# Stacking a three-term split of queries and keys: 12 copies inside the SBUF in place of 32 selection matmuls and four reads per batch

## The reference

```python
def _L0_xattn_ref(q, k, v, w_q, b_q, w_k, b_k, w_v, b_v, w_o, b_o):
    def proj(x, w, b):
        return (x @ w.T + b).reshape(B, S, N_HEADS, D_K).transpose(0, 2, 1, 3)
    qh = proj(q, w_q, b_q); kh = proj(k, w_k, b_k); vh = proj(v, w_v, b_v)
    scores = jnp.einsum('bhqd,bhkd->bhqk', qh, kh) / jnp.sqrt(D_K)
    attn = jax.nn.softmax(scores, axis=-1)
    out = jnp.einsum('bhqk,bhkd->bhqd', attn, vh).transpose(0, 2, 1, 3).reshape(B, S, D_MODEL)
    return out @ w_o.T + b_o
...
x = x + jnp.tanh(g_xattn[0]) * _L0_xattn_ref(_layernorm(x), ctx_1024, ctx_1024, ...)
x = x + jnp.tanh(g_ffn[0]) * _L0_ffn_ref(_layernorm(x), ...)   # 8 experts, top 2, silu(g) * u
```

## Time and profile before

| | before |
|---|---|
| median of 3 runs | 1110.66 us (1105.49 to 1113.64) |
| the profiled execution's own time | 1108.67 us |
| its span, first to last instruction | 1107.0 us |
| mean granted TensorE clock | 0.956 |
| PE, PEld busy share of the span | 91%, 78% |
| DVE, ACT, POOL busy share of the span | 55%, 46%, 33% |
| one iteration of the loop (MT to MT) | 24.86 us |

### The profile page before, as it was taken

How to read it: one execution, slowest core, us unless ns; L and a number is a source line. 1 busy time by engine, 2 the same in 40 slices (tenths; PEclk the granted TensorE clock), 3 DMA queues, 4 the chain that set the end, 5 groups by cost and what they waited for, 6 DMA issues and landing times.

```text
span 1107.0 us, 24925 instructions
## 1 busy us (share of the span) xinstructions
PE 1009.7 (91%) x8750; PEld 860.1 (78%) x8750; DVE 610.4 (55%) x1525; ACT 504.3 (46%) x800; POOL 365.1 (33%) x439
## 2 busy tenths in 40 slices
PE   5899999999999987738999999999889999999994
PEld 4566777777777754527899999999689999999993
DVE  3657777778777773533644444444354444444442
ACT  4467777777777764322433232322243232332321
POOL 1224545555555553424212122121222222121221
PEclk9899999999999996868999999999989999999997
DMA  8001111111111155475612121121262122121211
GB/s 249 21 21 30 42 41 40 45 55 49 40 40 49 40 211 209 157 241 151 237 29 38 20 39 25 34 35 24 41 232 39 20 39 34 24 39 20 39 28 23
DMA packets 48365, 77.20 MB, mean 70 GB/s; under 512 B 8768, under 2 KB 42176, under 8 KB 44480
## 3 DMA queue, kind: packets, MB, share of 16 engines
q0 software_dynamic: 18080, 50.15, 16.8%
q1 hardware_dynamic: 30240, 26.47, 8.4%
HBM read 52.07 MB, written 24.26 MB: 69 GB/s over the span
## 4 chain that ended last, share of the span: by engine, by line
PE 79%; ACT 5%; DVE 4%; issue 4%; POOL 3%; DMA 2%; SPq 1%; POOLq 0%; ACTq 0%; DVEq 0%
PE gate L1514 16%; PE up L1514 16%; PE down L1527 11%; PE down L1529 6%; PE pv L587 4%; PE scores L576 4%; PE misc L483 4%; PE scores L537 3%; PE maxps L551 2%; PE misc L510 2%; PE misc L519 2%; ACT probs L767 2%; POOL K_rest L1200 2%; PE misc L621 1%; PE turned L1455 1%
## 5 line engine op out<-in xcount | busy, mean ns | idle before, releaser
L1805 POOL DMA_INDIRECT out<-y,token x64 | 99.8, 1559 | 437.8 <-DVE y L1712 350.3
L1607 ACT ACTIVATE silu<-gate 128x512 f32<-128x512 f32 x128 | 76.5, 598 | 280.9 <-PE up L1514 280.9
L1514 PE MATMUL gate<-x_hi,w_split 128*128 128x256 f32 x1024 | 186.0, 284 | 6.5 <-DVE w_split L1686 4.5
L976 DVE TENSOR_REDUCE max_neg<-maxps 128x4 f32<-128x1024 f32 x128 | 156.4, 1222 | 57.5 <-PE maxps L551 57.5
L1527 PE MATMUL down<-w_split,h_hi 128*128 128x512 f32 x512 | 185.8, 398 | 0.0
L1514 PE MATMUL up<-x_hi,w_split 128*128 128x256 f32 x1024 | 185.4, 283 | 0.0
L1703 DVE TENSOR_TENSOR h<-silu,up 128x512 f32<-128x512 f32 x128 | 88.0, 688 | 176.4 <-ACT silu L1607 176.4
L767 ACT ACTIVATE probs<-scores 128x1024 f32<-128x1024 f32 x124 | 127.3, 1026 | 78.3 <-PE scores L576 77.2
L1514 PEld LDWEIGHTS gate<-x_hi,w_split 128*128 128x128 f32 x1024 | 150.6, 191 | 10.1 <-issue 6.8
L1514 PEld LDWEIGHTS up<-x_hi,w_split 128*128 128x128 f32 x1024 | 149.6, 190 | 0.0
L1529 PE MATMUL down<-w_split,h_lo 128*128 128x256 f32 x512 | 144.1, 282 | 0.0
(11 more groups left out here) (205 smaller groups left out, 1595.7 us busy)
## 6 DMA issues: line engine op xcount, KB each, us to landing
stage<-gate_T POOLq DMA_DIRECT2D x10, 1024.0 KB, 6.4
stage<-up_T POOLq DMA_DIRECT2D x10, 1024.0 KB, 8.4
stage<-down_T POOLq DMA_DIRECT2D x10, 1024.0 KB, 10.3
xg<-dispatched SPq DMA_DIRECT2D x34, 272.0 KB, 3.0
ctxT<-ctxT SPq DMA_DIRECT2D x17, 256.0 KB, 3.0
x_all<-x SPq DMA_DIRECT2D x16, 256.0 KB, 5.1
out<-x_all SPq DMA_DIRECT2D x16, 256.0 KB, 2.2
dispatched<-pads SPq DMA_DIRECT2D x4, 272.0 KB, 13.7
```

The source lines that it names most:

```text
L976: V.tensor_reduce(to, maxps[:], AX.X, ALU.max, negate=True).then_inc(s["max_taken"], 1)
L1514: last = mm(bank[:, i, :], weights(w, mat)[:, c, cols], x[:, c, :], start=m == 0, stop=m == len(terms) - 1)
L1607: nc.scalar.activation(silu[pair % 2][:], gate[pair % 2][:], ACT.Silu).then_inc(s_silu, 1)
L1805: pool.indirect_dma_start(out, bass.IndirectOffsetOnAxis(token[:, t:t + 1], axis=0), y[:, t, :], None, compute_op=ALU.add).then_inc(s_adde ...
```

## The change

For batches 2 to 15 the four units are gone from PE and ACT. SP copies instead: `stack` on SP issues three DMAs (one per term) for each half `c` of Q and of K, 12 per batch, each 128 partitions x 1 KB of `high` or `rest` into every fourth partition of `queries` or `keys`. For that the rows of a stack are interleaved (row 4 * dim + term, `STEP` = 4), the host permutes the columns of the Q and K weights, and the shift row is row 63. M0 to M7 now contract 63 rows, of which each fourth holds zeros. On SP the first halves stand between `store_residual` and `store_shift`, behind waits for S3 and for the splits of K and Q; the second halves stand behind `store_shift` and a wait for S7. M0 and M4 wait for the halves (`stacked`), and so does the next `split` on POOL.

Batches 0 and 1 are still stacked by matmuls, now with 128-row selection matrices that lie in `ctx_high` and `ctx_rest` until these are needed; they are 1 MB to load in place of 0.5 MB.

The order is changed too. PE: TX goes ahead of S4, Q behind M4, S5 and M5 behind Q, then RK and weigh 1. ACT: `read_k` and `norm_x` go ahead of the exponentials of S3, the read of TX behind them, `read_q` ahead of those of S5, the read of TX2 ahead of those of S7. DVE's and POOL's orders stay.

```diff
-SHIFT = 3 * DK
+TERMS = 3
+STEP = 4
+SHIFT = STACK - 1
...
-        FULL = ["V", "TO0", "TO1", "K", "TN", "WO", "TX", "RK", "Q", "TX2", "LG", "MT"]
+        FULL = ["V", "TO0", "TO1", "K", "TN", "WO", "TX", "Q", "RK", "TX2", "LG", "MT"]
...
+        def picks_of(what):
+
+            held = (c_high[0], c_high[1]) if what == "Q" else (c_rest[0], c_rest[1])
+            return [part[:].rearrange("p c s -> p (c s)") for part in held]
...
-            load(((probs[0][:, :, 0, :], pick_rows),), "picks_loaded")
+            load(((probs[0][:], pick_rows),), "picks_loaded")
...
+            def stack(what, c, to):
+
+                for term, part in enumerate((high, rest, high) if what == "Q" else (high, high, rest)):
+                    sp.dma_start(to[term::STEP, c * BLOCKS:(c + 1) * BLOCKS].bitcast(fp32),
+                                 part[what][:, c].bitcast(fp32)).then_inc(stacked[what][c], 16)
...
                 if back:
                     store_residual(b - 1, use)
+                if ahead:
+                    sp.wait_ge(s["unit_written"], unit(b, f"S{BLOCKS - 1}") + 1)
+                    sp.wait_ge(s["k_split"], b + 3)
+                    stack("K", 0, k[par])
+                    sp.wait_ge(s["q_split"], b + 3)
+                    stack("Q", 0, q[par])
                 if nxt:
                     store_shift(b + 1, 1 - par, use)
+                if ahead:
+                    sp.wait_ge(s["unit_written"], unit(b, f"S{HPAIRS - 1}") + 1)
+                    stack("K", 1, k[par])
+                    stack("Q", 1, q[par])
...
-                for i in range(QT):
-                    for part, source in (("high", high), ("rest", rest)):
-                        for half in range(HPP):
-                            r = slice(half * STACK, (half + 1) * STACK)
-                            last = mm(scores[:, half * QT + i, :], picks[f"{what} {part}"][r, i, :], source[what][r, c, :],
-                                      start=part == "high", stop=part == "rest")
+                for i in range(BLOCKS):
+                    for m, source in enumerate((high, rest)):
+                        last = mm(scores[:, i, :], picks_of(what)[m][:, i * P:(i + 1) * P], source[what][:, c, :], start=m == 0, stop=m == 1)
...
-                if pair == 0:
-
-                    pe.wait_ge(s["unit_read"], units)
+                if isinstance(b, int) and b < 2:
+                    if pair == 0:
+
+                        pe.wait_ge(s["unit_read"], units)
+                elif pair % BLOCKS == 0:
+                    for what in "KQ":
+
+                        pe.wait_ge(stacked[what][pair // BLOCKS], b * STACKED - STACKED)
...
                 if back:
                     attn_out(use)
+                if ahead:
+                    turn_x(b + 2, use)
                 score(b, par, 4)
                 max_of_next(4)
                 if ahead:
-                    turn_x(b + 2, use)
+                    project_q(use)
+                score(b, par, 5)
+                max_of_next(5)
                 if is_last(b):
                     use.read(pe, "KNOWN")
                 if late:
                     ranks(b - 2, use)
-                stack_ahead("K0")
                 weigh(b, par, 1)
-                max_of_next(5)
-                score(b, par, 5)
-                if ahead:
-                    project_q(use)
                 score(b, par, 6)
...
-                stack_ahead("K1")
                 if back:
                     logits(use)
                 if nxt:
                     turn_maxima(b + 1, use)
-                stack_ahead("Q0")
                 weigh(b, par, 3)
-                stack_ahead("Q1")
...
                 exps(b, 2)
+                if ahead:
+                    read_k(b + 2, use)
                 if back:
                     read_whole(oT[:], "TN", use)
+                if ahead:
+                    norm_x(b + 2)
                 exps(b, 3)
                 if ahead:
-                    read_k(b + 2, use)
-                    norm_x(b + 2)
+                    read_whole(xT[:], "TX", use)
                 exps(b, 4)
...
                 if ahead:
-                    read_whole(xT[:], "TX", use)
-                stack_ahead("K0")
+                    read_q(b + 2, use)
                 exps(b, 5)
                 if back:
                     norm_x2(b - 1, 1 - par)
                 read_pv(b, 1)
                 exps(b, 6)
-                if ahead:
-                    read_q(b + 2, use)
-                exps(b, 7)
                 if back:
                     read_whole(x2T[:], "TX2", use)
+                exps(b, 7)
                 read_pv(b, 2)
-                stack_ahead("K1")
                 if back:
                     sigmoid(use)
-                stack_ahead("Q0")
-                stack_ahead("Q1")
                 read_pv(b, 3)
...
+                if isinstance(b, int) and b == 2:
+                    alone.wait_ge(s["unit_written"], 2 * len(STACKS))
+                else:
+                    for done in stacked[what]:
+                        alone.wait_ge(done, b * STACKED - 2 * STACKED)
                 G.tensor_copy(high[what][:], dense[what][:]).then_inc(s["high_chain"], 1)
```

More of the change, by code:

```diff
@@ L158, in attention_stage @@
         rest = {what: sb(f"{what}_rest", [P, HC, SEQ], f32r) for what in "QK"}
-        picks = {what: sb(f"picks_{what}", [P, QT, P], f32r) for what in ("Q high", "Q rest", "K high", "K rest")}
         q = [sb(f"queries{i}", [P, HPAIRS, SEQ], f32r) for i in range(2)]
@@ L279, in read @@
                 eng.wait_ge(misc_read[n], uses + 1)
-        UNITS = ["S0", "S1", "S2", "S3", "S4", "K0", "S5", "S6", "S7", "K1", "Q0", "Q1"]
+        def picks_of(what):
+            held = (c_high[0], c_high[1]) if what == "Q" else (c_rest[0], c_rest[1])
+            return [part[:].rearrange("p c s -> p (c s)") for part in held]
+        UNITS = [f"S{pair}" for pair in range(HPAIRS)]
         STACKS = ["K0", "Q0", "K1", "Q1"]
+        STACKED = 16 * TERMS
         def units_before(b):
-            last = isinstance(b, int) and b == BATCHES - 1
-            return b * len(UNITS) + (2 * len(STACKS) if not last else len(STACKS))
+            return b * len(UNITS) + 2 * len(STACKS)
         def unit(b, what):
-            order = [n for n in UNITS if n not in STACKS] if isinstance(b, int) and b >= BATCHES - 2 else UNITS
-            return units_before(b) + order.index(what)
+            return units_before(b) + UNITS.index(what)
         def is_last(b):
@@ L863, in body @@
             def body(b, par, use, ahead, nxt, back, late):
-                def stack_ahead(what):
-                    if ahead:
-                        read_stack(par, what[0], int(what[1]), unit(b, what))
                 exps(b, 0)
@@ L1064, in vector_attention @@
             for n, what in enumerate("QK"):
-                for m, part in enumerate(("high", "rest")):
-                    last = V.tensor_copy(picks[f"{what} {part}"][:], probs[0][:, 2 * n + m, 0, :].rearrange("p (i c) -> p i c", i=QT))
+                for m in range(2):
+                    last = V.tensor_copy(picks_of(what)[m], probs[0][:, 2 * n + m].rearrange("p t s -> p (t s)"))
             last.then_inc(s["picks_ready"], 1)
@@ L1241, in body @@
                 if ahead:
[L1242 removed]
+                    split(b + 2, "Q", use)
                 if late:
@@ L1259, in gpsimd_attention @@
             return scatter_next_to_last, scatter_last
-        handed = dict(over=attention_over, s=s, units=units_before(BATCHES - 1) + sum(n not in STACKS for n in UNITS))
+        handed = dict(over=attention_over, s=s, units=units_before(BATCHES - 1) + len(UNITS))
         return sync_attention, tensor_attention, scalar_attention, vector_attention, gpsimd_attention, handed
```

24 lines of the change are left out of this document (9 added, 15 removed).

## The result

The changed kernel takes **1133.25 us** (median of 4 runs, 1131.22 to 1135.36), the kernel before 1109.48 on the same chip: ratio **1.0221, 95% interval 1.0182 to 1.0259**. It is slower, by about 2%. The profiled execution took 1135.24 us, its span is 1133.6 (before 1107.0), its mean granted clock 0.934 (before 0.956).

The account below looks back on a forecast made before the run. PE looked the bound (24.29 of 24.86 us busy), but tied with DVE's chain at M1. 1108.67 - 8.4 - 0.9 - 3.0 + 2.0 = 1098.4, or 1100.4 from the median; forecast the middle, 1099.4 us, range 1088 to 1114.

Parts of the forecast that it names:

- The walk: Loop, engine by engine from MT to MT: 24.86 us falls to 24.15, 0.7 per iteration, 8.4 over twelve.
- On DVE nothing is taken away.: DVE's chain behind MT: its steps stay, V comes 1.4 us earlier, so M0 begins at 5.12, M1 at 6.40.
- The transfers at nothing: SP's twelve stack DMAs per iteration: costed at nothing, 0 to 0.7 us per iteration in the range.
- The warning on K of iteration 1: Iterations 0 and 1: 1.5 us gain each, 3.0 together, since K may wait for batch 3's context behind six transfers.
- Prologue: Before the loop: 0.5 MB more to load and eight units without 64-row concurrency lose 2.0 us, from 0.5 to 4.
- Iteration 14 was to gain 0.9: Iteration 14: with S0 at 3.65 us, the chain to M0 shortens by about 0.9 us.
- Slower, 1135: Rival at S0 and M1: PE's clock falls twice per iteration, 27.25 us each, 1135 us in all; chance 0.12.
- Falls seldom, 6 us: Rival in the loop: PE's clock falls in a third of iterations, 4 x 1.5 = 6 us, 1105; chance 0.17.
- The signs named: Profile if right: no L537, MT to MT 24.0 to 24.3, S0 and M1 wait 0.7 us, PE near 21, clock 1.00.
- signs of being wrong: Loop profile: clock below 1.00, M0 or M4 waiting for DMA, M1 without a wait, or MT to MT below 23.5.

Follow-up runs that it names:

- q_split_late: The changed kernel with POOL's split of Q held until DVE has done the positions of the same iteration; 1104.74 us, 0.9976 of the kernel before.
- short_copies: The changed kernel with each stack transfer copying 16 of its 256 columns, so later batches' scores use stale columns; 1129.65 us, 1.0193 of the kernel before.
- best_a: q_split_late plus batch 3's context loaded in iteration 0 and DVE's prologue fills moved behind the rests of K and Q; 1098.12 us, 0.9905 of the kernel before.
- old_order: The changed kernel, stacking by transfers, with PE and ACT in the order of the kernel before; 1126.80 us, 1.0172 of the kernel before.
- ctx_split_moved: The changed kernel with POOL's context split and output bias moved to the next iteration; 1119.12 us, 1.0101 of the kernel before.

## Why the prediction was wrong

**The walk itself held.** In the short iteration from 282.89, S0 waits 0.73 us (0.7 predicted), M1 is at 6.45 (6.40), M5 at 17.04 (16.98); only behind the positions does M7 come at 23.12 for 22.3, having waited 0.86 for the held DVE. The walk gave MT to MT at 24.15 us; q_split_late, the change with one wait more on POOL, has 23.99. Of 3.2 us taken from PE, 2.3 turn into waits (2.5 predicted). The wait moved, though: in q_split_late Q's issues stand ahead of the shift on SP, S0 waits 1.1 to 1.7 us for it, and that takes up M1's wait for DVE.

**The step that failed: "On DVE nothing is taken away."** True of its instructions, wrong of their lengths. The walk took every DVE duration as fixed, and moved Q's split on POOL without asking beside what it would come to stand. The prediction had both times: `read_q` ends at 17.6, 2 us for POOL's split, so to 19.6; DVE's positions from 18.7 on. It set that split only against SP's issues. And rows of the hold were in the trace of before, at 93.71. Worth 12.2 us for the positions and 15.1 for the first choice with its clock: 27.3 where the forecast had nothing, against a gain of 11.8 without the holds (8.4 forecast; 1.1 of the 11.8 is iteration 2's own hold, gone).

**The transfers at nothing: right for bytes and landings in the loop** (short_copies, no wait at M0 or M4 there), wrong in iteration 14, where M4 waits 1.51 us for a copy that lands late beside the weight loads, and wrong for the queue. The warning on K of iteration 1 was the right mechanism; it was sized at part of 3 us and took 3.6 alone, so that iterations 0 and 1 gave nothing instead of 3.0 (best_a: 3.6). In the old order the same issues push the shift back.

**Prologue:** a loss of 2.0, bounds 0.5 to 4, in place of the 6.0 in this execution; 2.4 to 5.1 in the eight other traces with this prologue. It has two parts that the rows tell apart. The selection matrices' load is issued at 4.82 us in every trace and lands at 11.8 to 13.6 us in these nine, for 8.9 to 10.2 in the three with the prologue of before. In the pair above, DVE's copies of them begin 3.1 us later, 1.2 of it was DVE's spare time that the prediction saw, and K's rest is 1.9 us later. From K's rest to the first MT it takes 28.2 us here for 24.1; in the nine traces this goes with how long the clock is low ahead of the first MT, 25.5 us with 3.8 us low, 26.4 to 26.7 with 6.8 to 7.3 (as long as before), 27.3 to 27.4 with 10.2, 28.2 with 13.7. So at equal clock the stretch with the eight units is some 2.4 us longer than before, and about 1.7 are this execution's clock; neither was isolated. Why behind the last MT 4.2 us are added (-0.2 to 5.0 in those), 2.8 of them among the experts, whose code is unchanged, stays open; the clock is low for 66.7 us among the experts here and for 60.2 before. Iteration 14 was to gain 0.9 and lost 0.7, M4's wait among it; in four of those traces it gained 0.5 to 1.8.

**The rivals.** "Slower, 1135" met the number by another road. Its clock falls are real (the loop's clock is 0.94), but those that cost come behind a held DVE, and are 6 of 27 us; in q_split_late the clock is 1.00 with waits of up to 1.69 us ahead of S0. "Falls seldom, 6 us" has its like in old_order, 6.6 us. (Added up from its own terms, faster has 0.44 and slower 0.15, not 0.45 and 0.14.)

**The signs named.** Met: no L537, the waits of S0 and M1, DVE's waits for M5 to M7 lower by 0.84 (1.20 for 2.04). Not met: MT to MT, clock 1.00, PE's busy time (22.4, not 21). Of the signs of being wrong, the clock showed, and an M4 that waits for a DMA in iteration 14. None of them was a DVE duration.

## What to carry to other kernels

Before moving a step of GpSimd, or whatever sets its start, lay its new time beside VectorE's order and look for small steps on SBUF operands; a step of 0.17 us can take 1.2, and where the walk was tied here, its 1.05 us cost 1.0. Compare busy time per engine at equal instruction counts: where an engine's steps became longer at the same shapes, look for what holds it. And when durations depend on alignment, first remove the meetings, then measure anything else.

## What was not expected of the hardware

**What holds L1006 is not the scatter alone.** L1006 is held to the end of an indirect DMA's step (the scatter, 0.96 us on POOL), but not by that step alone. In all 14 traces together, 60 two-input steps of the first choice begin 0.36 to 0.68 us into a scatter with `ctx_high` directly behind it on POOL, and all 60 are held, to 0.01 to 0.03 us behind the scatter's recorded end. Begun up to 0.3 us into it they are free (66 of 66). Where another scatter or idle time follows instead, 169 such steps begun 0.44 to 0.8 us into a scatter take 0.17 to 0.18 us, all of them. In ctx_split_moved, where the context's split is elsewhere, L1006 begins 0.45 us into the last scatter, as it does at 309.98 in the changed kernel, and is free:

```profile
201.04 0.17 DVE L1006 TENSOR_TENSOR t<-bids,v 128x16 f32<-128x16 f32 x1
```
```profile
200.59 0.96 POOL L1218 DMA_INDIRECT dispatched<-row,posi  x1 [0.30 <-issue]
```

So this hold comes with the context's split behind the scatter; which part of POOL's work it is, is not shown.

**The scatter itself holds L1002**, a tensor-scalar step with one SBUF input: begun 0.59 to 0.69 us into it, it ends within 0.03 us of its end (0.24 to 0.35 us for 0.15), and begun up to 0.43 us into it, it is free. A reduction (L1009, one input) begun at 0.46 us isn't held. This is what splits even from odd iterations, which start the first choice 0.16 us apart: L1002 is held by 0.2 us in the even one from 307.83, and that brings L1006 to 0.45 us into the last scatter; in the odd one from 282.89 it stands 0.05 us into it.
